# Attention's output ahead of the transposes of later rows in stage 1, with VectorE's order to match

## The reference, cut to what matters

```python
out_swa = _swa(x_in, wq, wk, wv, wo)              # 4 heads, window of 128 rows, softmax
pred = silu(k_flat @ w1.T + b1) @ w2.T + b2       # k_flat = x_in, 256 -> 1024 -> 256
loss = 0.5 * sum((pred - v_flat) ** 2)            # v_flat = out_swa
upd = (1 - alpha) * p - theta * grad(loss)        # for p in w1, b1, w2, b2
out_mem = mlp(upd, k_flat)                        # in the next stage, with the stepped weights
```

## Time and profile before

| | |
|---|---|
| median of 3 runs | 1840.76 us (1838.13 to 1840.92) |
| the profiled execution | 1840.37 us |
| its span, first to last instruction | 1838.2 us |
| mean granted TensorE clock | 0.993 of full speed |
| stage 1 in the span | up to about 715 us |
| matmuls in the whole program | 12168, PE busy 1794.2 us (98%) |

### The profile page before, as it was taken

One profiled execution on the slowest core, in us unless ns is written; L12 is line 12 of the kernel. 1 busy time (PEld: TensorE's weight loads), 2 busy tenths in 40 slices (PEclk: granted clock), 3 DMA queues, 4 the chain that ended last, 5 costly groups with the idle time before them and its releaser, 6 DMA issues.

```text
span 1838.2 us, 35720 instructions
## 1 busy us (share of the span) xinstructions
PE 1794.2 (98%) x12168; PEld 1578.6 (86%) x12168; DVE 1214.8 (66%) x2253; ACT 947.9 (52%) x1792; POOL 935.5 (51%) x699
## 2 busy tenths in 40 slices
PE   7999999999999999999999999999999999999995
PEld 5788888888888887788788887889999999999995
DVE  7977777777777776766677668644555555555552
ACT  7666666666666665634545444343444434444341
POOL 6565666656666664046566666554233323332234
PEclk9999999999999999999999999999999999999998
DMA  6211111111111102220111103167898888888884
GB/s 239 69 39 36 38 37 35 38 35 35 55 39 35 39 28 81 70 74 17 47 46 47 47 12 109 39 227 254 291 286 288 283 279 281 289 289 283 284 278 96
DMA packets 141023, 234.16 MB, mean 127 GB/s; under 512 B 24757, under 2 KB 88972, under 8 KB 140817
## 3 DMA queue, kind: packets, MB, share of 16 engines
q1 hardware_dynamic: 116368, 220.50, 35.0%
q0 software_dynamic: 24576, 12.69, 4.6%
HBM read 194.58 MB, written 78.45 MB: 149 GB/s over the span
## 4 chain that ended last, share of the span: by engine, by line
PE 53%; DMA 3%; issue 1%; DVE 1%; POOL 0%; ACT 0%; SPq 0%; POOLq 0%; DVEq 0%; ACTq 0%
PE bank L86 26%; PE bank L2048 22%; PE bank L1312 4%; DMA out_rows<-c_y_rest,c_token_rest 2%; DMA c_w<-in_e1T 1%; PE bank L2270 1%; PE bank L1811 1%; DMA slots<-last_row,last_index 1%; POOL out_rows L2222 0%; POOL slots L2007 0%; PE bank L2281 0%; SPq L2104 0%; DVE c_y_rest L2189 0%; DVE early L1690 0%; POOLq L2356 0%
## 5 line engine op out<-in xcount | busy, mean ns | idle before, releaser
L2048 PE MATMUL bank<-c_xT,c_w 128*128 128x160 f32 x3072 | 429.9, 299 | 3.7 <-DMA c_w<-in_e1T 3.0
L2048 PEld LDWEIGHTS bank<-c_xT,c_w 128*128 128x128 f32 x3072 | 419.3, 190 | 5.0 <-DMA c_w<-in_e1T 3.4
L2007 POOL DMA_INDIRECT slots<-b_row,b_index x224 | 251.2, 1121 | 194.3 <-issue 116.4
L2222 POOL DMA_INDIRECT out_rows<-c_y,c_x x64 | 100.1, 1564 | 376.2 <-DMA out_rows<-c_y_rest,c_token_rest 275.1
L2170 DVE TENSOR_TENSOR c_gT<-bank,c_sil 128x480 f32<-128x480 f32 x128 | 84.2, 658 | 212.0 <-PE bank L2048 212.0
L2138 ACT CAST c_gTs_high<-c_gT 128x384 fp32r<-128x384 f32 x128 | 65.6, 513 | 135.3 <-DVE c_gT L2170 135.3
L2131 ACT ACTIVATE c_sil<-bank 128x480 f32<-128x480 f32 x128 | 73.1, 571 | 110.7 <-PE bank L2048 110.2
L2163 DVE TENSOR_TENSOR c_gTs_low<-c_gT,c_gTs_high 128x384 fp32r<-128x384 f32 x128 | 71.6, 560 | 74.8 <-ACT c_gTs_high L2138 74.8
L485 POOL TENSOR_TENSOR last_row<-last_row,a_e 128x256 f32<-128x256 f32 x33 | 53.5, 1620 | 124.5 <-DVE a_e L783 124.5
L86 PE MATMUL bank<-c_w2s_high,c_gTs_high 128*128 128x256 f32 x384 | 114.0, 297 | 0.9 <-DVE c_gTs_low L2163 0.9
L86 PE MATMUL bank<-c_w2s_high,c_gTs_low 128*128 128x256 f32 x384 | 106.9, 278 | 0.0
(11 more groups left out here) (346 smaller groups left out, 5451.0 us busy)
## 6 DMA issues: line engine op xcount, KB each, us to landing
c_w<-in_e1T SPq DMA_DIRECT2D x64, 1536.0 KB, 7.0
c_w<-in_e2T SPq DMA_DIRECT2D x48, 768.0 KB, 9.0
early<-in_e2T SPq DMA_DIRECT2D x16, 768.0 KB, 8.7
slots<-a_fill SPq DMA_DIRECT2D x16, 642.0 KB, 3.9
c_x<-slots SPq DMA_DIRECT2D x64, 160.5 KB, 8.6
a_x_in<-in_x SPq DMA_DIRECT2D x32, 128.0 KB, 2.0
xT_tiles<-a_xT SPq DMA_DIRECT2D x32, 128.0 KB, 1.7
swaT_tiles<-a_oT SPq DMA_DIRECT2D x32, 128.0 KB
```

The costliest lines, as they stand in the source:

```text
L2007: pool.indirect_dma_start(out=T["slots"], out_offset=bass.IndirectOffsetOnAxis(ap=index[:, t, k:k + 1], axis=0), in_=row[:, t, :], in_offs ...
L2048: return nc.tensor.matmul(out, lhsT, rhs, start=first, stop=last, skip_group_check=True)
L2222: pool.indirect_dma_start(out=T["out"], out_offset=bass.IndirectOffsetOnAxis(ap=token, axis=0), in_=rows, in_offset=None, bounds_check=las ...
```

## The change

On TensorE, in the tiles from 2 on, `turn_x(n + 2, p)` moves from ahead of attention's output to behind it, so the order is: transposes of h, attention's output, transposes of the rows of tile n+2, pred. Tile 1 keeps its order. On VectorE, in the tiles from 2 on, `part_prob` and `grad_z` move ahead of `modulate`, so `modulate` stands straight ahead of the low parts of the turned hidden layer. No instruction, wait, buffer or transfer is added or removed.

```diff
@@ VectorE, body
                     gather_dW(n - 2, dW1T if p else dW2, (1, 2, 3, 4))
+                    part_prob(n, p)
+                    grad_z(n - 1)
                     if ahead(n):
                         modulate(n + 2, p)
-                    part_prob(n, p)
-                    grad_z(n - 1)
                 for g in range(2):
                     dve.wait_ge(S("hT_high"), 2 * n + g + 1)
@@ TensorE, body
                 if first:
                     turn_x(1, 1)
-                elif ahead(n):
+                elif not known(n, 2):
                     turn_x(n + 2, p)
...
                 ins.then_inc(S("o_mm"), 1)
+                if known(n, 2) and ahead(n):
+                    turn_x(n + 2, p)
                 wait_past(pe, S("dz"), 2 * n - 1)
```

## The result

The changed kernel takes 1851.91 us (median of 6 runs, 1848.95 to 1853.86), the kernel before 1840.93 us (6 runs beside them). The ratio is 1.006 with a 95% interval of 1.0048 to 1.0072: slower by 11.0 us. The prediction was 1849.2 us, slower, within 1846.0 to 1852.5. The profiled execution took 1851.5 us, its span is 1849.3 us, 11.1 more than before.

A forecast was written before the change was run, and what follows sets the result against it. TensorE's own instruction stream was taken as the bound, waiting for almost nobody. A late low half costs 28 x 0.30 + 0.17 = 8.6 us on 1840.4 to 1840.8, giving 1849.2 us, range 1846.0 to 1852.5.

The forecast's parts named there:

- What bounds, and no wait to remove: Stage 1: TensorE's instruction stream is the bound; the swapped instructions' operands lie ready for over a microsecond.
- The chain on VectorE: After grad_z's second half at 0.43, modulate delays the first low half from 1.48 to 1.93 after the tile's zero.
- The rule on emptied pipelines: VectorE: next operation starts only once the pipeline is empty; links 0.69 and 0.42, loss 0.47 a tile, about 1854.
- the longer chain: Rival on VectorE: links without overlap add 0.17 a tile, 13.5 us slower in all, 1853.9 us; chance 0.10.
- The handover and the loss at pred: Pred's second pass starts 0.34 after the low half's end, at 2.96 instead of 2.66: 0.30 us a tile lost.
- The lead of 0.26: Today's time from the low half's end (323.63) to pred's start (323.89), which the change spends by delaying it 0.45.
- Nothing behind it costs: ScalarE and VectorE copies behind the moved parts start 0.45 to 0.8 later; idle of 1.85 and 1.60 us covers them.
- The sum: 28 tiles of 0.30 plus 0.17 for tile 3: 8.6 us slower, 1849.2 us.
- The upper end of the forecast: 0.39 a tile, 11.2 us: VectorE starts later by register waits, or TensorE pays 0.09 entry to narrow products again.
- the 8.6: Predicted total loss in us at pred over the 29 tiles with modulate.
- list of signs: Expected profile: VectorE idle 0.57 before grad_z's second half, low half 1.93, second pass 2.96, tile pairs 0.60 longer, stall under line 897.

The follow-up runs named there:

- TensorE's part alone: Against the kernel before: only turn_x moved behind attention's output, VectorE's order as before; 1841.62 us against 1840.83, ratio 1.0005.
- the delay without the reorder: Kernel before plus one unused 512-column VectorE reduction behind grad_z in tiles 2 to 30, both old orders kept; 1852.21 us against 1840.83, ratio 1.0065.
- The kernel with 256 columns more: Kernel before plus one unused 256-column VectorE reduction behind grad_z in tiles 2 to 30; 1844.43 us against 1840.13, ratio 1.0022.
- the second trace: The changed kernel profiled once more, unchanged; one execution, 1850.03 us.
- VectorE's part alone: Against the kernel before: modulate moved behind part_prob and grad_z, turn_x still ahead of attention's output; 1875.67 us against 1840.83, ratio 1.0197.

## Why the prediction was right

*What bounds, and no wait to remove.* Right. TensorE's part alone changes nothing that can be measured, and the earlier masks buy nothing in any kernel here.

*The chain on VectorE.* Right in every link: 0.43, 1.04, 1.60, 1.94 against 0.43, 1.03, 1.59, 1.93. Tiles 31 and 32, which had no modulate, had shown the wait of grad_z before it existed in the others. The two experiments that move modulate ahead of that wait, by one instruction or two, give the whole loss back, and the delay without the reorder brings a loss of the same size: the cause is shown from both sides.

*The rule on emptied pipelines.* In the changed kernel modulate starts at 327.09, while the grad_z instruction ahead of it ends at 326.48 + 0.69 = 327.17. Read as whole recorded lengths, the rule in the Trainium skill's section "The DRAIN you can't avoid" in "VectorE: DVE Perf Modes" would have the start behind that end; the same section adds that an operation that is not held starts earlier, and the trace is in line with that. The measurement decides: the two links are 327.09 - 326.48 = 0.61 and 327.99 - 327.65 = 0.34, and the longer chain did not come.

*The handover and the loss at pred.* Right: second pass at 2.96 against 2.96, 0.30 a tile. The lead of 0.26 that the prediction names is not free as a whole, since the handover to pred's first pass takes 0.15 of it. The kernel with 256 columns more shows that: its low half is only 0.20 late, and pred is held already. The prediction's sum used the right figure, 0.15 to the second pass.

*Nothing behind it costs.* Right for the moved copies: VectorE still idles 1.77 ahead of line 934, where it had 1.60. On ScalarE:

```profile
328.83 0.37 ACT L509 COPY a_xT<-bank 128x256 f32<-128x256 f32 x1 [0.83 <-PE bank L991]
...
332.68 0.37 ACT L665 COPY a_swa<-bank 128x256 f32<-128x256 f32 x1 [1.22 <-PE bank L270]
```

The copy of the turned rows waits 0.83 for the moved transposes and starts 0.96 later against the tile's zero (328.83 - 326.05 = 2.78 for 323.28 - 321.46 = 1.82), where the prediction had about 0.8. The idle time ahead of line 665 shrinks from 1.85 to 1.22. The cover was needed and it held.

*The sum.* Too small by 2.4 us, and this is the term that was mis-sized: "Nothing else in the tile waits, so nothing absorbs it: PE's whole later stream shifts" took every other distance of TensorE as unchanged. Two were not. Pred's passes of tile 15 in the changed kernel:

```profile
351.73 0.28 PE L86 MATMUL bank<-w2T_low,pair_high 128*128 128x256 f32 x1
...
354.44 0.81 PE L270 MATMUL bank<-a_woT,a_oT 128*128 128x256 f32 x3
```

From the second pass to the next group, 23 distances, it takes 354.44 - 351.73 = 2.71, 0.118 each, while tile 14 takes 331.62 - 329.01 = 2.61. In the first trace 9 of the 29 tiles are like tile 15; in the second trace 16 are. The other term is spread over hidden layer, gradient and backward product, about 0.02 each, of which the products of queries and keys give 0.01 back: 0.05 a tile. The backward passes of tile 14 show it. Their second one in the kernel before:

```profile
319.17 0.40 PE L86 MATMUL bank<-a_w2n_low,a_eT_high 128*128 128x512 f32 x1
```

And in the changed kernel:

```profile
323.74 0.40 PE L86 MATMUL bank<-a_w2n_low,a_eT_high 128*128 128x512 f32 x1
```

From the second pass to the last it is 321.46 - 319.17 = 2.29 and 326.05 - 323.74 = 2.31. The whole of the 29 tiles goes from the last backward pass of tile 2 to that of tile 31. In the kernel before the first of them is

```profile
66.71 0.39 PE L86 MATMUL bank<-a_w2n_high,a_eT_low 128*128 128x512 f32 x1
```

and in the changed kernel the two are

```profile
67.09 0.39 PE L86 MATMUL bank<-a_w2n_high,a_eT_low 128*128 128x512 f32 x1
...
690.16 0.39 PE L86 MATMUL bank<-a_w2n_high,a_eT_low 128*128 128x512 f32 x1
```

That is 679.08 - 66.71 = 612.37 before and 690.16 - 67.09 = 623.07 after, 10.7 more. Of it 8.4 are the stalls, 1.0 pred's longer passes and 1.3 the rest. The other 0.4 of the span's 11.1 lies ahead of tile 2 (67.09 for 66.71), where the traces of the other kernels differ by more than that from each other.

Some of the hit is luck. The upper end of the forecast, 11.2 us, was built from two things that did not come, later starts on VectorE or the entry into the narrow products paid once more; the loss of 11.0 lies near that end because of passes that the prediction took as unchanged. By the time alone the 8.6 is just outside the interval of the loss (8.8 to 13.3 us); it is the second pass of pred that shows the 0.30 to be right. Why the other passes became longer is not shown. The granted clock isn't the reason: it is 1.00 of full speed (2.4 GHz) in these tiles in both traces.

Of the prediction's list of signs two did not come as told: the stall is not listed under line 897, and pairs of tiles grew by 0.7 to 0.8 and not by 0.60, for the longer passes just told. What comes behind kept its length: from the zero of tile 32 to the end of the span it is 1139.7 us, before 1139.6.

## What to carry to other kernels

Look for tiles at the ends of a loop in which the step that you want to move is missing: they run the new order already, and their waits are those that the others will get. When an instruction is moved behind another that waits, it inherits that wait, and so does everything queued behind it; a place ahead of the wait, in the idle time that the same move has opened, can be free. Where the bounding engine waits for nothing, look for the smallest lead of its operands, less the handover, since that is what a reorder spends.

## What the runs showed of the hardware

The handover from VectorE to a TensorE that waits for it is the same everywhere here. In every tile in which the changed kernel or the one with 512 columns more holds pred, its first pass starts 0.15 and its second 0.34 after the recorded end of the low half; tile 14 of the changed kernel has 328.81 and 329.01 behind 327.99 + 1.28 - 0.60 = 328.67.

TensorE's distances between equal passes have two values each: 0.113 or 0.118 for 256 columns in pred, and 2.287 or 2.313 for the backward product from its second pass to its last, ten distances. In the two kernels with an added instruction, which hold TensorE at pred, most tiles have the longer distance in pred and the shorter one in the backward product; in the changed kernel and in the four that move parts of it, the backward product has the longer one in most tiles. That includes the kernel with VectorE's part alone, whose TensorE stream is that of the kernel before, so the order of TensorE's instructions isn't the cause. Nor is the granted clock: in eight of the ten traces it is 1.00 of full speed (2.4 GHz) in all these tiles, and in the other two it falls once, for 3.4 us. What is stays open. The longer distance in pred is seen only where TensorE was held ahead of it: tile 3 alone among the tiles up to 30 has it in the kernel before, none has it with TensorE's part alone. But being held isn't enough for it, since 20 of the 29 held tiles of the changed kernel's first trace run pred at the shorter distance throughout or for most of its passes.
